# Cross-attention over 16 batches on one Trainium2 core: K and Q projected in transposed form and stacked through DRAM

## The chip, the cores and the metric

The kernel runs on one NeuronCore of a Trainium2 chip, as one launch. The metric is the device time of the launch in microseconds (us), lower is better. The core has a matrix engine (PE, with its weight loads shown apart as PEld), a vector engine (DVE), a scalar engine (ACT), a GpSimd engine (POOL), and a sync engine (SP) that issues most DMA transfers. Each engine runs its own instructions in the order in which they are written; semaphores carry the waits between engines and for transfers.

## The reference

There are 16 batches of 128 query rows (C = 160 channels, 20 heads of D = 8) and 128 context rows (E = 256), of which 124 are text tokens and 4 are image-prompt (IP) tokens. Cut to what matters, for each batch:

```python
q = heads(x @ W_q); k_t = heads(text @ W_k); v_t = heads(text @ W_v)
probs_t = softmax(q k_t^T * D**-0.5); text_out = probs_t v_t
k_ip = heads(ip @ W_k_ip); v_ip = heads(ip @ W_v_ip)
qsem = l2norm(probs_t @ text); sem = qsem . l2norm(ip)
probs_ip = softmax(q k_ip^T * D**-0.5 + 0.5 * sem) * spatial_mask
out = (text_out + probs_ip v_ip) @ W_out + b_out + x
```

## The kernel before, in words

**Windows.** All engines run `windows(...)`: window b = -1 to 18, one per batch, each made of G = 5 groups of HG = 4 heads. Windows 4 to 13 are a hardware loop of pairs; n = 1 - p is the buffer of the next batch, p that of this one. In window b, PE computes the scores of batch b (L706, one matmul of 512 columns for a group: `q_stack` holds 4 heads stacked on 128 partitions, `k_diag` the K of the 4 heads on a block diagonal), transposes the probabilities of two groups back (L723), and multiplies those of three groups back by V and by the Gram matrix of the context (L746, L748, `main_rhs`, from which the norm of qsem comes). DVE takes the row maxima (L627, L628) and the sums of products (L608, L610), ACT the exponentials (L497) and the copy of the transposed probabilities (L466). The IP branch of the batches before runs on POOL: a power for the norm (`rnorm`, L429, the last thing in POOL's window), then in the next window `fused` (L369, L373), the IP output (L248, L253, L256), `text` (L379), `ip_stage` (L385), a copy of IP columns (L389), `centred` (L394), sums, the V columns (L409, L410), `rip_masked` and `ip_probs` (L419, L423). The power waits for `clamped` of DVE (L556), made in group 4.

**K and Q before.** fp32 values are split in a high and a low fp32r part, so that one fp32r matmul with a contraction over 4 heads x 8 channels x 4 products gives the exact scores. In window b, for batch b + 1: PE computes Gram, V and K with the tokens on the partitions (L686, 12 instructions) and Q (L758, 4); ACT copies the high parts (L448, L503), DVE subtracts to get the low parts (L633, L565); PE turns `k_split` and `q_split` with an identity (L765, L775, L713, L714); ACT copies the turned data out of PSUM (L485, L453, L458, L459) into `k_stack` and `q_stack`; SP spreads `k_stack` to the diagonal with eight transfers (L314, L324). `k_diag` and `q_stack` are needed at the score matmul of group 0 in window b + 1.

**SP's order** in a window: IP rows of K (L292), context and x of batch b + 2 (L297, L299), residual rows and V of the IP tokens (L303, L306), `k_diag` groups 0 to 3 (L314), `main_rhs` (L319), `k_diag` group 4 (L324), the output (L329). SP is one in-order queue: a wait holds up every transfer behind it. The work ahead of the windows (the prologue) loads the weights, normalises the IP tokens and projects their K and V; window -1 makes K and Q of batch 0 on chip.

## Time and profile before

| | |
|---|---|
| median of 3 runs | 233.72 us (233.47 to 237.01) |
| profiled execution, device time | 234.08 us |
| its span in the trace | 232.0 us |
| granted PE clock, mean share of full | 0.958 |
| PE busy | 207.8 us, 90% |
| DVE / ACT / POOL busy | 190.8 / 170.0 / 154.4 us |
| DMA, share of 16 engines | 44.6% |

The span is what the trace covers; the device time is 2.1 us longer. "Busy" counts an instruction from start to end, and matmuls overlap in the pipeline, so the chain of waits, where each piece is counted once, gives the truer PE durations. A line number is that of the kernel before unless the text says that it is one of the changed kernel.

### The profile page before, as it was taken

To read this page: it belongs to the slowest core of one execution; us is meant where nothing else is said; L and a number is where in the kernel's file an instruction comes from. 1 tells how busy PE (TensorE), PEld (TensorE's weight loads), DVE (VectorE), ACT (ScalarE), POOL (GpSimd) and SP (SyncE) were. 2 spreads that over 40 slices of the span, in tenths; PEclk is the share of its full clock that TensorE was granted. 3 is DMA by queue.
4 is the path that set the end of the run, shared out by engine and by line. 5 is a ranking of instruction groups with operands and counts; after the bars stand their busy time and mean duration, and the time that the engine had idled before them with its cause. 6 is when DMAs were issued, how large, how long until landed. Compare 5 with 4: busy or idle time off the path is not lost.

```text
span 232.0 us, 6889 instructions
## 1 busy us (share of the span) xinstructions
PE 207.8 (90%) x1562; PEld 192.6 (83%) x1562; DVE 190.8 (82%) x1149; ACT 170.0 (73%) x561; POOL 154.4 (67%) x263
## 2 busy tenths in 40 slices
PE   1948989999999999999999999999999999988433
PEld 1647879998898999999999999999999999977222
DVE  5753778796979798998979897989798979998862
ACT  2063978897978798897969797988888888975000
POOL 5611003649596868788796969696969696979650
PEclk9976999999999999999999999999999999999955
DMA  5405433465355545373736353646454553533030
GB/s 150 124 18 154 104 101 66 124 172 142 104 160 143 149 132 163 87 206 82 204 80 186 104 172 99 167 119 158 132 152 144 145 149 106 143 87 85 1 100 14
DMA packets 46348, 28.57 MB, mean 123 GB/s; under 512 B 7897, under 2 KB 43898, under 8 KB 46330
## 3 DMA queue, kind: packets, MB, share of 16 engines
q1 hardware_dynamic: 46330, 28.38, 44.6%
q8 instruction: 6, 0.10, 0.2%
q14 instruction: 12, 0.10, 0.1%
HBM read 11.11 MB, written 1.52 MB: 54 GB/s over the span
## 4 chain that ended last, share of the span: by engine, by line
PE 61%; DMA 9%; DVE 8%; POOL 7%; ACT 6%; issue 4%; SPq 3%; DVEq 0%; POOLq 0%; ACTq 0%
PE main_ps L746 11%; PE main_ps L748 11%; PE probsT_ps L723 10%; PE pa L686 9%; DMA main_rhs<-g_stage 6%; PE score_ps L706 6%; PE pb L732 5%; POOL rnorm L429 3%; PE pb L758 3%; PE pa L765 2%; ACT probs L497 2%; DVE junk L608 2%; PE pa L775 2%; SPq L324 1%; PE pb L695 1%
## 5 line engine op out<-in xcount | busy, mean ns | idle before, releaser
L497 ACT ACTIVATE probs<-score_ps,negmax 128x124 f32<-128x124 f32 x320 | 93.3, 413 | 0.7 <-DVE negmax L628 0.6
L608 DVE CUSTOM_DVE_ANT_0 junk<-main_ps,probs 128x124 f32<-128x124 f32 x320 | 78.0, 281 | 2.3 <-PE main_ps L748 1.5
L746 PE MATMUL main_ps<-main_rhs,probsT 124*128 124x137 f32 x320 | 65.1, 284 | 1.5 <-DVE small L610 1.4
L748 PE MATMUL main_ps<-main_rhs,probsT 124*128 124x137 f32 x320 | 63.3, 279 | 0.0
L429 POOL TENSOR_TENSOR rnorm<-clamped,exponent 128x20 f32<-128x20 f32 (+1 forms) x16 | 54.8, 3427 | 1.1 <-DVE clamped L556 1.1
L628 DVE TENSOR_REDUCE negmax<-score_ps 128x4 f32<-128x496 f32 x80 | 53.1, 664 | 0.0
L466 ACT ACTIVATE probsT<-probsT_ps 124x512 f32<-124x512 f32 x80 | 51.1, 639 | 2.8 <-PE probsT_ps L723 2.0
L746 PEld LDWEIGHTS main_ps<-main_rhs,probsT 124*128 124x128 f32 x320 | 48.9, 190 | 3.5 <-issue 2.6
L748 PEld LDWEIGHTS main_ps<-main_rhs,probsT 124*128 124x128 f32 x320 | 48.7, 188 | 0.0
L723 PE MATMUL probsT_ps<-ident_sb,probs 128*124 128x128 f32 x320 | 48.2, 273 | 0.0
L723 PEld LDWEIGHTS probsT_ps<-ident_sb,probs 128*124 128x124 f32 x320 | 38.4, 139 | 5.2
L706 PE MATMUL score_ps<-k_diag,q_stack 128*128 128x512 f32 x80 | 39.0, 488 | 0.3 <-ACT probs L497 0.3
L627 DVE COPY ip_score<-score_ps 128x16 f32<-128x16 f32 x80 | 13.3, 166 | 21.4 <-PE score_ps L706 21.4
L610 DVE COPY small<-main_ps 128x26 f32<-128x26 f32 x160 | 28.8, 180 | 0.0
L608 DVE DVE_READ_ACCUMULATOR2_ANT norm<- 128x1 f32 x320 | 26.6, 83 | 0.2 <-issue 0.2
L444 ACT ACTIVATE g_stage<-pa 128x128 f32<-128x128 f32 x16 | 4.4, 278 | 26.5 <-PE pa L686 16.4
L686 PE MATMUL pa<-wkv_sb,ctxT_sb 128*128 128x160 f32 x128 | 21.9, 319 | 0.0
L399 POOL TENSOR_TENSOR ip_exp_half<-ip_exp 128x40 f32<-128x40 f32 x16 | 4.0, 253 | 25.7 <-ACT ip_exp L491 25.7
L686 PEld LDWEIGHTS pa<-wkv_sb,ctxT_sb 128*128 128x128 f32 x128 | 19.8, 208 | 0.0
L248 POOL TENSOR_TENSOR ip_prod<-vrep,ip_probs 128x640 f32<-128x640 f32 x13 | 18.3, 1404 | 0.0
L409 POOL TENSOR_TENSOR main_rhs<-v_stage,one 124x80 f32<-124x80 f32 x16 | 5.1, 321 | 18.9 <-PE main_ps L748 8.9
L732 PE MATMUL pb<-wout_sb,oT 96*128 96x160 f32 x64 | 14.2, 349 | 2.9 <-DVE oT L620 2.9
(91 smaller groups left out, 339.2 us busy)
## 6 DMA issues: line engine op xcount, KB each, us to landing
main_rhs<-g_stage SPq DMA_DIRECT2D x16, 660.0 KB, 4.1
vrep<-vip_d SPq DMA_DIRECT2D x16, 320.0 KB, 3.5
k_diag<-k_stack SPq DMA_DIRECT2D x60, 64.0 KB, 2.1
ctxT_sb<-ctxT SPq DMA_DIRECT2D x16, 124.0 KB, 2.6
xT_sb<-xT SPq DMA_DIRECT2D x16, 80.0 KB, 2.0
xn_sb<-xn SPq DMA_DIRECT2D x16, 80.0 KB, 2.0
out<-out_sb SPq DMA_DIRECT2D x16, 80.0 KB, 1.7
k_diag<-k_stack SPq DMA_DIRECT2D x60, 16.0 KB, 2.0
```

Source lines behind the costliest of these rows:

```text
L429: pool.tensor_tensor(rnorm[:, heads], clamped[:, heads], exponent[:, heads], ALU.pow).then_inc(s_rnorm, 1)
L466: act.activation(probsT[tp][:, :, :].rearrange("t h s -> t (h s)"), probsT_ps[tp][0:T, :], ACT.Copy).then_inc(s_probsT, 1)
L497: last = act.activation(probs[p][:, h, :], score_ps[(p * G + g) % 2][:, j * TOK:j * TOK + T], ACT.Exp, bias=negmax[p][:, h:h + 1])
L608: dve.tensor_tensor_reduce(junk[:, 2 * r + a, :], u, probs[wb][:, h, :], 1.0, 0.0, ALU.mult, ALU.add, norm2[wb][:, h:h + 1])
L610: dve.tensor_copy(small[wb][:, PG * gg + r, :], main_ps[r][:, T:T + SMALL]).then_inc(s_norm, 1)
L628: dve.tensor_reduce(negmax[p][:, HG * g:HG * g + HG], sc[:, :, 0:T], AX_X, ALU.max, negate=True).then_inc(s_max, 1)
L686: mm = pe.matmul(pa[:, lo:lo + width], ctxT_sb[n][:, c, :], r, start=(c == 0), stop=(c == EC - 1))
L706: pe.matmul(score_ps[(p * G + g) % 2][:, :], q_stack[p][:, g, :], k_diag[p][:, g, :, :].rearrange("r h t -> r (h t)"), start=True, stop=Tr ...
L723: mm = pe.transpose(probsT_ps[tp][0:T, j * S:(j + 1) * S], probs[tb][:, HG * tg + j, :], ident_sb[:, :])
L732: mm = pe.matmul(pb[:, 0:C], oT[:, c, :], wout_sb[:, c, :], start=(c == 0), stop=(c == 1))
L746: pe.matmul(main_ps[r][:, 0:MAIN], probsT[mp][:, 2 * r, :], blk[:, RW - MAIN:RW], start=True, stop=True)
L748: pe.matmul(main_ps[r][:, MAIN:2 * MAIN], probsT[mp][:, 2 * r + 1, :], blk[:, 0:MAIN], start=True, stop=True).then_inc(s_main, 1)
```

## The change

- The projections of K and Q now have the weight as the stationary operand and produce channels on the partitions and tokens in the columns, in two halves of 80 channels (`project_k`, `project_q`). They run in group 4 of window b for batch b + 2, into the PSUM bank `pb`. Gram and V (`gram_and_v`) run in group 1 for batch b + 1. The output projection moves to bank `pa`.
- In group 0 of window b, one ACT copy and one DVE subtraction of 80 x 512 make the high and low parts of K and Q of batch b + 1 (`kq_split`). POOL's new `k_columns` writes the four IP columns of K into it, behind `ip_stage` in POOL's order.
- SP stores `kq_split` to DRAM (`store_k` two transfers, `store_q` four), then, after `ctxT` and `xT`, waits for these stores and loads the stacked forms back (`load_k` four transfers to the diagonal, `load_q` one). All of this is in window b, for batch b + 1.
- Gone are the turns on PE, the ACT copies of turned and doubled data, the DVE subtractions on doubled data, the K rows through `kip_d`, and window -1. The prologue is written in a new order; ACT issues two of the weight loads and, for batch 0, `store_q` and `load_q`.

```diff
+        def store_k(eng, n):
+
+            for x in range(2):
+                src = kq_split[:, x, :, :].rearrange("p a t -> p (a t)").bitcast(F32)
+                eng.dma_start(k_d[n, x * CH:(x + 1) * CH, :, :],
+                              src.unsqueeze(1).broadcast_to([CH, 2, 2 * TOK])).then_inc(s_kst, 16)
+
+        def store_q(eng, n):
+
+            for x in range(2):
+                for a in range(2):
+                    eng.dma_start(q_d[n, x * CH:(x + 1) * CH, :, a * S:(a + 1) * S],
+                                  kq_split[:, 2 + x, :, :].bitcast(F32)).then_inc(s_qst, 16)
+
+        def stacked_rows(dram, n, j, rows):
+
+            return bass.AP(dram.tensor, dram.offset + n * G * HG * ROWS * TOK + j * ROWS * TOK,
+                           [[TOK, rows], [HG * ROWS * TOK, G], [1, TOK]])
+
+        def load_k(sp, n):
+            for j in range(HG):
+                sp.dma_start(k_diag[n][ROWS * j:ROWS * (j + 1), :, j, :].bitcast(F32),
+                             stacked_rows(k_d, n, j, ROWS)).then_inc(s_kd[n], 16)
+
+        def load_q(sp, n):
+            sp.dma_start(q_stack[n][:, :, :].bitcast(F32), stacked_rows(q_d, n, 0, HG * ROWS)).then_inc(s_qd[n], 16)
...
                 n = 1 - p
+                if w == 1:
+                    sp.wait_ge(s_vip, 1)
+                    sp.dma_start(vip_d, vip_sb[:, :]).then_inc(s_vip_out, 16)
                 if has(w) and has(w, ahead=1):
 
-                    wait(sp, s_kT, b + 1)
-                    wait(sp, s_kq4, b + 1)
-                    sp.dma_start(k_split[T:TOK, :, :, :, :].rearrange("t h c a d -> t (h c a d)").bitcast(F32),
-                                 kip_d[bass.ds((b + 1) * NIP, NIP), :]).then_inc(s_kip_in, 16)
+                    wait(sp, s_kcol, b + 2)
+                    store_k(sp, n)
+                    store_q(sp, n)
                 if has(w) and has(w, ahead=2):
 
-                    wait(sp, s_ctx_mm, b + 1)
-                    sp.dma_start(ctxT_sb[p][:, :, 0:T], ctxT[b + 2]).then_inc(s_ctx_in[p], 16)
-                    wait(sp, s_q_mm, b + 1)
-                    sp.dma_start(xT_sb[p][0:CH, :, :], xT[b + 2]).then_inc(s_xT_in[p], 16)
+                    wait(sp, s_gv_mm, b + 1)
+                    sp.dma_start(ctxT_sb[p][:, :, NIP:TOK], ctxT[b + 2]).then_inc(s_ctx_in[p], 16)
+                    sp.dma_start(xT_sb[p][:, :, :], xT[b + 2]).then_inc(s_xT_in[p], 16)
+                if has(w) and has(w, ahead=1):
+
+                    wait(sp, s_kst, 32 * (b + 2))
+                    load_k(sp, n)
+                    wait(sp, s_qst, 64 * (b + 2))
+                    load_q(sp, n)
                 if has(w, lag=2):
 
...
+                if has(w) and has(w, ahead=1):
 
...
+                    sp.dma_start(main_rhs[n][:, :, D + 1:D + 1 + WIN],
+                                 g_stage[:, :].unsqueeze(1).broadcast_to([TOK, NPAIR, WIN])).then_inc(s_grep[n], 16)
...
+            def ip_columns(b, p):
+
+                cols = bass.AP(ctxT_sb[p], 0, [[EC * WIN, 128], [WIN, EC], [TOK, 2], [1, NIP]])
+                src = ipunitT[:, :, bass.ds(b * NIP, NIP)].unsqueeze(2).broadcast_to([128, EC, 2, NIP])
+                pool.tensor_copy(cols, src).then_inc(s_ipcol, 1)
+
+            def k_columns(b):
+
+                pool.tensor_copy(kq_split[:, 0:2, :, T:TOK].bitcast(F32),
+                                 kip_split[:, :, :, bass.ds(b * NIP, NIP)].bitcast(F32)).then_inc(s_kcol, 1)
+
...
+                if has(w) and has(w, ahead=1):
+                    wait(pool, s_lo, b + 3)
+                    k_columns(b + 1)
                 if has(w) and has(w, ahead=2):
-                    wait(pool, s_ctx_mm, b + 1)
-                    pool.tensor_copy(ctxT_sb[p][:, :, T:TOK],
-                                     ipunitT[:, :, bass.ds((b + 2) * NIP, NIP)]).then_inc(s_ipcol, 1)
+                    wait(pool, s_gv_mm, b + 1)
...
-                    if g == 0 and has(w, ahead=1):
-
-                        wait(act, s_ctx_mm, b + 2)
-                        if w is None or w >= 0:
-                            wait(act, s_grep[p], 16 * (i + 1))
-                        act.activation(g_stage[:, NIP:NIP + TOK], pa[:, 0:TOK], ACT.Copy)
-                        act.activation(g_stage[:, 0:NIP], pa[:, T:TOK], ACT.Copy).then_inc(s_gstage, 1)
+                    if g == 0 and has(w) and has(w, ahead=1):
+
+                        wait(act, s_kq_mm, b + 3)
+                        wait(act, s_kst, 32 * (b + 1))
+                        wait(act, s_qst, 64 * (b + 1))
+                        act.activation(kq_split[:, :, 0, :], pb[0:CH, :].rearrange("p (x t) -> p x t", x=4),
+                                       ACT.Copy).then_inc(s_hi, 1)
+                    if g == 2 and has(w) and has(w, ahead=1):
+
+                        wait(act, s_gv_mm, b + 2)
+                        wait(act, s_grep[p], 16 * (i + 1))
+                        gv_stage()
                         wait(act, s_vcopy, b + 1)
-                        act.activation(v_stage[:, :], pa[0:T, TOK:TOK + C], ACT.Copy)
-                        act.activation(k_split[0:T, :, :, 0, :], doubled(pa[0:T, TOK + C:TOK + 2 * C]),
-                                       ACT.Copy).then_inc(s_khi, 1)
-                    if g == 3 and has(w) and has(w, ahead=1):
-
-                        wait(act, s_qT, b + 2)
-                        act.activation(q_stack[n][:, 0:G - 1, :].rearrange("r g t -> r (g t)"), pa[:, :],
-                                       ACT.Copy).then_inc(s_qst03, 1)
-                    if g == 4 and has(w) and has(w, ahead=1):
-
-                        wait(act, s_kq4, b + 2)
-                        act.activation(k_stack[:, G - 1, :], pb[:, 0:TOK], ACT.Copy)
-                        act.activation(q_stack[n][:, G - 1, :], pb[:, TOK:TOK + S], ACT.Copy).then_inc(s_st4, 1)
+                        v_stages()
...
-                    if g == 1 and has(w, ahead=1):
-
-                        wait(act, s_kT, b + 2)
-                        if w is None or w >= 0:
-                            wait(act, s_kd03[p], 64 * (i + 1))
-                            wait(act, s_kd4[p], 64 * (i + 1))
...
-                        else:
-                            act.activation(k_stack[:, 0:G - 1, :].rearrange("r g t -> r (g t)"), pa[:, :],
-                                           ACT.Copy).then_inc(s_kst03, 1)
...
+                    if g == 0 and has(w) and has(w, ahead=1):
+
+                        wait(dve, s_hi, b + 3)
+                        dve.tensor_tensor(kq_split[:, :, 1, :], pb[0:CH, :].rearrange("p (x t) -> p x t", x=4),
+                                          kq_split[:, :, 0, :], ALU.subtract).then_inc(s_lo, 1)
                     if has_group(w, g, 4):
...
+            def project_k(bank, n, width):
+
+                for x in range(2):
+                    for c in range(EC):
+                        mm = pe.matmul(bank[0:CH, x * TOK:x * TOK + width], wk_sb[:, c, x * CH:(x + 1) * CH],
+                                       ctxT_sb[n][:, c, NIP:NIP + width], start=(c == 0), stop=(c == EC - 1))
+                return mm
+
+            def project_q(bank, lo, n):
+
+                for x in range(2):
+                    for c in range(2):
+                        mm = pe.matmul(bank[0:CH, lo + x * S:lo + (x + 1) * S], wq_scaled[:, c, x * CH:(x + 1) * CH],
+                                       xT_sb[n][:, c, :], start=(c == 0), stop=(c == 1))
+                return mm
+
+            def gram_and_v(n):
+
+                for lo, width, r in ((0, WIN, ctxT_sb[n]), (WIN, C, wv_sb)):
+                    for c in range(EC):
+                        mm = pe.matmul(pa[0:T, lo:lo + width], ctxT_sb[n][:, c, NIP:TOK], r[:, c, :],
+                                       start=(c == 0), stop=(c == EC - 1))
+                return mm
+
+            pe.wait_ge(s_ctx_in[0], 16)
...
                         if g == 0:
-                            wait(pe, s_kd03[p], 64 * (i + 1))
-                            wait(pe, s_qst03, b + 1)
-                        if g == G - 1:
-                            wait(pe, s_kd4[p], 64 * (i + 1))
+                            wait(pe, s_kd[p], 64 * (i + 1))
+                            wait(pe, s_qd[p], 16 * (i + 1))
...
                             pe.matmul(main_ps[r][:, MAIN:2 * MAIN], probsT[mp][:, 2 * r + 1, :], blk[:, 0:MAIN],
                                       start=True, stop=True).then_inc(s_main, 1)
-                    if g == 0 and has(w, ahead=1):
-
-                        if w == -1:
-                            wait(pe, s_wq, 1)
-                        wait(pe, s_xT_in[n], 16 * (i + p + 1))
+                    if g == 4 and has(w) and has(w, ahead=2):
+
+                        wait(pe, s_ctx_in[p], 16 * (i + 2))
+                        wait(pe, s_xT_in[p], 16 * (i + 2))
+                        wait(pe, s_ipcol, b + 3)
+                        wait(pe, s_lo, b + 3)
+                        project_k(pb, p, TOK)
+                        project_q(pb, 2 * TOK, p).then_inc(s_kq_mm, 1)
+                    if g == 1 and has(w) and has(w, ahead=1):
+
                         wait(pe, s_final, b - 3)
-                        wait(pe, s_st4, b + 1)
-                        for c in range(2):
-                            mm = pe.matmul(pb[:, 0:C], xT_sb[n][:, c, :], wq_scaled[:, c, :], start=(c == 0), stop=(c == 1))
-                        mm.then_inc(s_q_mm, 1)
-                    if g == 1 and has(w, ahead=1):
-
-                        wait(pe, s_klo, b + 2)
-                        wait(pe, s_kip_in, 16 * (b + 2))
-                        for k in range(G - 1):
-                            mm = pe.matmul(pa[:, k * TOK:(k + 1) * TOK], stacked(k_split, k), ident_r_sb[:, :],
-                                           start=True, stop=True)
-                        mm.then_inc(s_kT, 1)
-                    if g == 2 and has(w, ahead=1):
-
-                        wait(pe, s_qlo, b + 2)
-                        if w != -1:
-                            wait(pe, s_kst03, b + 2)
-                        bank_q = main_ps[1] if w == -1 else pa
-                        for k in range(G - 1):
-                            mm = pe.matmul(bank_q[:, k * S:(k + 1) * S], stacked(q_split, k), ident_r_sb[:, :],
-                                           start=True, stop=True)
-                        mm.then_inc(s_qT, 1)
+                        wait(pe, s_vstage, b + 1)
+                        gram_and_v(n).then_inc(s_gv_mm, 1)
```

On SP, in the last window ahead of the loop (window 3; the loop has the same order), the kernel before issues, with its waits:

```order
L292 DMA k_split<-kip_d 4x640 [waits s_kq4,s_kT]
L297 DMA ctxT_sb<-ctxT 128x2x124 [waits s_ctx_mm]
L299 DMA xT_sb<-xT 80x256 [waits s_q_mm]
L303 DMA xn_sb<-xn 128x160
L306 DMA vrep<-vip_d 128x640
L314 DMA k_diag<-k_stack 32x4x128 [waits s_kst03,s_scores]
L314 DMA k_diag<-k_stack 32x4x128 x3
L319 DMA main_rhs<-g_stage 128x10x132 [waits s_gstage,s_main]
L324 DMA k_diag<-k_stack 32x128 [waits s_st4]
L324 DMA k_diag<-k_stack 32x128 x3
L329 DMA out<-out_sb 128x160 [waits s_final]
```

and the changed kernel at the same place (its own line numbers):

```order
L256 DMA k_d<-kq_split 160x1x256 [waits s_kcol]
L256 DMA k_d<-kq_split 160x1x256
L263 DMA q_d<-kq_split 160x1x128 x4
L316 DMA ctxT_sb<-ctxT 128x2x124 [waits s_gv_mm]
L317 DMA xT_sb<-xT 80x256
L273 DMA k_diag<-k_d 32x5x128 [waits s_kst]
L273 DMA k_diag<-k_d 32x5x128 x3
L277 DMA q_stack<-q_d 128x5x128 [waits s_qst]
L329 DMA xn_sb<-xn 128x160
L332 DMA vrep<-vip_d 128x640
L339 DMA main_rhs<-g_stage 128x10x132 [waits s_gstage,s_main]
L344 DMA out<-out_sb 128x160 [waits s_final]
```

The first transfer of SP's window now waits for POOL's `k_columns` (`s_kcol`), twelve transfers stand ahead of and up to the arrival of `q_stack`'s, and a window issues 17 where it issued 14.

On POOL, in the middle of the first window of the loop, the kernel before has (REGISTER_ALU and ISA are bookkeeping of the loop):

```order
L256 TENSOR_TENSOR ip_out<-ip_half 128x160 [waits s_attn,s_ipout]
L379 TENSOR_TENSOR text<-small,rden 128x160 [waits s_attn]
L240 REGISTER_ALU
L240 REGISTER_ALU [waits s_max]
L385 TENSOR_TENSOR ip_stage<-ip_score,one 128x80 [waits s_fuse]
L240 REGISTER_ALU
L389 ISA [waits s_ctx_mm]
L389 COPY ctxT_sb<-ipunitT 128x2x4
L394 TENSOR_TENSOR centred<-fused,ipmax 128x80 [waits s_ipmax]
```

and the changed kernel:

```order
L250 TENSOR_TENSOR ip_out<-ip_half 128x160 [waits s_attn,s_ipout]
L414 TENSOR_TENSOR text<-small,rden 128x160 [waits s_attn]
L234 REGISTER_ALU
L234 REGISTER_ALU [waits s_max]
L420 TENSOR_TENSOR ip_stage<-ip_score,one 128x80 [waits s_fuse]
L234 REGISTER_ALU
L368 ISA [waits s_lo]
L368 COPY kq_split<-kip_split 80x4x4
L364 ISA [waits s_gv_mm]
L364 COPY ctxT_sb<-ipunitT 128x2x2x4
L431 TENSOR_TENSOR centred<-fused,ipmax 128x80 [waits s_ipmax]
```

The copy that releases SP's stores stands where the copy of the context's IP columns stood, behind the power of the window before and the whole IP output.

## Rows read from the trace of the kernel before

**Rows 1.** Windows view: stretch, busy us (instructions) by engine, granted clock, DMA.
```profile
core 0: us, PE busy (x) PEld busy (x) DVE busy (x) ACT busy (x) POOL busy (x), PEclk, DMA share, GB/s
103.33:115.36 12.03, 12.03 (x100) 11.57 (x99) 10.86 (x73) 10.49 (x37) 9.69 (x17) 1.00 0.54 144
```

**Rows 2.** Chain of waits from 103 us: start us, us, engine, tile, line.
```profile
103.33 1.53 PE pa L686 x12
104.87 0.23 PE score_ps L706
...
106.48 0.55 PE pb L758 x4
...
108.63 0.40 PE pa L765 x4
109.03 0.28 PE score_ps L706
...
110.68 0.40 PE pa L775 x4
...
113.80 0.06 PE pb L713
113.86 0.11 PE pb L714
...
115.36 1.53 PE pa L686 x12
116.90 0.23 PE score_ps L706
```

**Rows 3.** Timeline of window 8: start us, us, engine, line, operation.
```profile
124.85 0.11 DVE L556 TENSOR_TENSOR clamped<-norm,guard 128x20 f32<-128x20 f32 x1
125.41 3.54 POOL L429 TENSOR_TENSOR rnorm<-clamped,exponent 128x20 f32<-128x20 f32 x1
```

**Rows 4.** Timeline, SP's issues and POOL's column copy, same window.
```profile
118.91 0.64 SPq L297 DMA_DIRECT2D ctxT_sb<-ctxT  x1
...
119.74 0.45 SPq L299 DMA_DIRECT2D xT_sb<-xT  x1
...
120.44 0.35 SPq L303 DMA_DIRECT2D xn_sb<-xn  x1
...
121.24 0.19 POOL L389 COPY ctxT_sb<-ipunitT 128x8 f32 x1
...
121.90 2.60 SPq L314 DMA_DIRECT2D k_diag<-k_stack  x4
```

**Rows 5.** DMA view, issues by tile: count, KB each, median us to landing.
```profile
main_rhs<-g_stage SPq DMA_DIRECT2D x16, 660.0 KB, 4.1
vrep<-vip_d SPq DMA_DIRECT2D x16, 320.0 KB, 3.5
k_diag<-k_stack SPq DMA_DIRECT2D x60, 64.0 KB, 2.1
xT_sb<-xT SPq DMA_DIRECT2D x16, 80.0 KB, 2.0
```

**Rows 6.** Lines view: shapes, count, busy us, mean ns, idle before.
```profile
L453 ACT ACTIVATE q_stack<-pa 128x512 fp32r<-128x512 f32 x15 | 10.0, 667 | 0.0
L633 DVE TENSOR_TENSOR k_split<-pa,k_split 124x320 fp32r<-124x320 f32 x16 | 7.8, 489 | 4.4 <-ACT k_split L448 4.4
```

**Rows 7.** Timeline of PE: first score matmul of windows 0, 3 and 15.
```profile
19.64 0.83 PE L706 MATMUL score_ps<-k_diag,q_stack 128*128 128x512 f32 x1
...
54.16 0.50 PE L706 MATMUL score_ps<-k_diag,q_stack 128*128 128x512 f32 x1
...
199.71 0.48 PE L706 MATMUL score_ps<-k_diag,q_stack 128*128 128x512 f32 x1
```

**Rows 8.** Windows view of short stretches; columns as in Rows 1.
```profile
14.00:15.00 1.00, 0.30 (x3) 0.16 (x2) 0.56 (x2) 0.95 (x3) 0.00 (x0) 0.71 0.00 0
...
34.00:35.00 1.00, 0.00 (x0) 0.00 (x0) 1.00 (x9) 0.00 (x0) 0.00 (x0) 1.00 0.79 203
```

More of the change, by code:

```diff
@@ L36 @@
 CH = C // 2
-CP = 96
+CR = CH + 1
+WIN = NIP + TOK
+ROWS = 4 * D
 HG = 4
@@ L211, in xattn_program @@
         block = ctx.enter_context(nc.Block())
-        def doubled(cols):
-            r = cols.rearrange("t (h d) -> t h d", d=D)
-            return r.unsqueeze(2).broadcast_to([r.shape[0], H, 2, D])
         def windows(eng, window):
-            for w in range(-1, 4):
+            for w in range(4):
                 window(w, w % 2, w // 2, w)
@@ L675, in window @@
                     grp = b * G + g
-                    if g == 0 and has(w, ahead=1):
-                        wait(pe, s_ctx_in[n], 16 * (i + p + 1))
-                        wait(pe, s_ipcol, b + 2)
-                        if w == 0:
-                            wait(pe, s_kst03, 1)
-                        wait(pe, s_qst03, b + 1)
-                        for lo, width, rhs in ((0, TOK, None), (TOK, C, 0), (TOK + C, C, C)):
-                            for c in range(EC):
-                                r = ctxT_sb[n][:, c, :] if rhs is None else wkv_sb[:, c, rhs:rhs + C]
-                                mm = pe.matmul(pa[:, lo:lo + width], ctxT_sb[n][:, c, :], r, start=(c == 0), stop=(c == EC - 1))
-                        mm.then_inc(s_ctx_mm, 1)
                     if g == 3 and has(w, lag=3):
```

312 lines of the change are left out of this document (154 added, 158 removed).

## The prediction

> **What bounds the kernel now.** I read the windows view first, to see whether one engine is full: from 103 to 115 us, one window, PE is busy throughout, at full clock, and DVE, ACT and POOL have about 1.2, 1.6 and 2.4 us of slack in 12 [rows 1]. Then the chain of waits, to see what the window is made of. It has nothing but PE from one L686 group to the next: 115.36 - 103.33 = 12.03 us [rows 2]. So the body is PE-bound, and from the score matmul of window 3 (54.16) to that of window 15 (199.71) it takes 145.55 us, 12.13 a window [rows 7]. Ahead of window 0 lie 19.6 us, behind the start of window 15 another 232.0 - 199.7 = 32.3 us, where the power on POOL and the output of the last batches run down.
>
> The other thing to read is how late K and Q of the next batch may come. Now they never leave the chip's engines except for the spread to `k_diag`. The question for the changed kernel is whether its longer way, POOL, SP, DRAM and back, still ends before the next window's first score matmul.
>
> **PE, what goes and comes.** Gone in a window: L686 1.53, Q 0.55, turns 0.40 + 0.40 + 0.06 + 0.11, together 3.05 us [rows 2]. L686's 12 instructions stream 4 x 128 + 8 x 160 = 1792 columns in 1.53 us, 0.85 ns a column. The new ones: K 8 x 128, Q 8 x 128, Gram 4 x 132, V 4 x 160 = 3216 columns, 2.75 us. Net -0.30 us. Two score matmuls behind the turns cost 0.28 instead of 0.23 in the same chain; taken as gone too, a full PE would need 12.03 - 0.4 = 11.65 us, call it 11.7.
>
> **ACT and DVE.** ACT loses seven copies and gains one of 80 x 512, as L453's 0.67 us; DVE loses two of 0.49 us and gains one of 512 columns, about 0.7 [rows 6]. Neither was the bound, so both are costed at nothing; PE's 12.03 us hides them.
>
> **The way of K and Q, which sets the window.** T is the start of a window's first score matmul (116.90 for window 8, 104.87 for window 7, from the chain [rows 2, 4]). Step by step:
> 1. T to `clamped` on DVE: 124.96 - 116.90 = 8.1 us; the power starts at 125.41, T + 8.5 [rows 3]. Nothing that the change removes lies between PE's third group and DVE's fourth except 0.05s.
> 2. The power, 3.54 us, then `fused` twice, the IP output, `text`, `ip_stage`. The column copy behind them starts at 121.24, that is 121.24 - 104.87 = 16.4 us behind the T of the window before [rows 4]. `k_columns` stands at this very place. I take 16.2, since DVE has one subtraction less in the way, plus 0.2 for the copy itself.
> 3. SP: six stores, `ctxT`, `xT`, four loads, and only then the load of `q_stack`. Four static issues of `k_diag` take 2.60 us, 0.65 each; `ctxT` to `xT` is 0.83, `xT` to `xn` 0.70 [rows 4]. Six stores at 0.63 make 3.8, then 1.5, then 2.6, with gaps 8.0 us. The two waits on stores cost nothing: the last store is issued 3.2 us in and needs about 2.0 to land, as `xT`, while SP is busy with issues until 7.9 us.
> 4. Landing of `load_q`, 320 KB in 512-byte pieces. No row shows that shape. `vrep` with 320 KB takes 3.5; on the line from `xT` (80 KB, 2.0) to `main_rhs` (660 KB, 4.1, pieces of 528 bytes) it would be 2.9 [rows 5]. I take 3.2, plus 0.1 to PE.
>
> Sum: 16.2 + 0.2 + 8.0 + 3.3 = 27.7 us. It leads from T of window b to T of window b + 2, since the power that it contains is that of window b and the copy stands in window b + 1. Two PE-bound windows last 23.4. So the way is 4.3 us too long, and it is a loop: a later T makes a later `clamped`. The window becomes 27.7 / 2 = 13.85 us, with PE idle for 2.15 us ahead of each first score matmul. What else could be late then is not: `ctxT` for the group-4 projection is issued 4.0 us behind the copy, about T + 6.7, and is wanted at T + 10.
>
> The Trainium skill, "DMA: Bandwidth & Descriptors", section "Anatomy of one DMA", gives 2.0 us fixed plus the bytes at 436 GB/s for a transfer (measured on the GpSimd path); by that estimate `load_q` would land in 2.75 us instead of 3.2, and the result would be some 3 us lower. Its "Rules for kernel authors" says that under 64 KB one pays mostly overhead, which speaks against cutting this way in 12 transfers; the trace agrees in that 64 KB takes 2.1 us and 660 KB only 4.1 [rows 5].
>
> **The prologue.** First issues are spread over two queues, so the first K projection should start near 3.5 us (one issue of about 0.6 and a landing of 2 to 3 [rows 4, 5] behind the start), `k_columns` near 7.4 behind eleven short steps on PE, ACT, DVE and POOL, stores to 8.7, loads of K to about 13; ACT stores Q from 9 and can load it only at 13.2, with a landing of 3.3. First score matmul about 16.5 us instead of 19.64 [rows 7]. Window 1 needs `k_columns` in window 0 (16.7) + 8.0 + 3.3 = 28.1, window 2 about 39.3, window 3 the first power: 28.1 + 8.5 + 3.6 + 1.6 + 0.2 + 11.3 = 53.2, against 54.16 now. The gain at the start is thus used up but for 1 us.
>
> **Sum.** Windows 3 to 15: 12 x 13.85 = 166.2 against 145.55, +20.6 us. Start -1.0. Behind T of window 15 POOL is no longer behind, -0.8. Span 232.0 + 18.8 = 250.8, device time 252.9. The profiled execution was 0.4 us above the median of the runs (234.08 against 233.72), so 252.5 in terms of the median; I say 253.
>
> **Rivals.**
> - *The load comes in time (faster).* The way takes under 23.4 us, PE stays full at 11.7 a window. Then T of window 3 is near 51.5, window 15 at 51.5 + 12 x 11.7 = 192, and the time 192 + 32.3 + 2.1 = 226 us. It decides at 23.4 us: step 3 and 4 together would have to be 7.0 us instead of 11.3. SP's short issues take 0.45 (`xT`'s own [rows 4]); ten of those, 1.5 for `ctxT` and `xT` and 2.9 for landing are 4.5 + 1.5 + 2.9 = 8.9. So only with an error in steps 1 and 2 as well. 10 in 100.
> - *Shorter issues, half the stall.* With these 8.9 us the way is 25.3, the window 12.7, and the time T3 = 49.5, + 152 + 31.5 + 2.1 = 235 us: within 2% of before. 10 in 100.
> - *The clock falls as well.* PE's granted clock fell to a mean of 0.71 in the microsecond from 14 us, in which PE was busy for 0.3 us, but it stayed at 1.00 through an idle microsecond at 34 to 35 us [rows 8]. If 2.1 us of idling in every window brings it down to 1.2 GHz for some of the following groups, PE's three groups in step 1 (5.8 us at full clock) take up to 1.7 us more, the way 29.1 to 29.4, the window 14.6, the time about 262 us. 20 in 100. The Trainium skill, "TensorE: Matmul & The Clock Gate", section "HAM oscillation", describes just this, a kernel that waits for a transfer in each tile and runs cold each time; the row at 34 us shows one short wait that did not do it.
> - *DMA engines fill up.* The change adds about 1 MB to some 1.8 MB a window; they are 54% busy now [rows 1], so about 80% after. Not a bound, but landing may rise by a few tenths: inside the range.
>
> **How the numbers follow.** My forecast, stall of about 2 us a window with full clock, 60 in 100: 246 to 258. Low end of the whole 237, near the second rival, high end 262 by the clock. Faster by over 2% 0.10, within 2% 0.10, slower 0.80 (2% is about what a measurement of this kernel can tell from no change).
>
> **What would show it.** Right: the window lasts 13.5 to 14.2 us; PE's longest wait is at the score matmul of group 0, for DMA `q_stack<-q_d`, about 2 us, 12 or more times; on SP the issue of `q_d`'s load stands 7.5 to 8.3 us behind `k_columns`; and `k_columns` starts 16 us behind T of the window before. Wrong: PE full in the middle at 11.7 us a window; or `k_columns` much earlier than the power lets it, or issues on SP well under 0.6 us, or another engine at the end of PE's waits. The first score matmul should be near 16.5 us.

## The result, and the profile after

| | before | changed kernel |
|---|---|---|
| median | 234.26 us (4 runs, 233.47 to 237.01) | 297.13 us (4 runs, 294.72 to 297.56) |
| span of the profiled execution | 232.0 us | 295.3 us |
| PE busy | 207.8 us, 90% | 222.9 us, 75% |
| granted PE clock, mean | 0.958 | 0.932 |

The ratio is 1.268 (95% interval 1.258 to 1.277). The sign was forecast, the size was not: 297 us lies far outside 237 to 262.

The page of the changed kernel, its busy times, the shares of the chain, and two groups with the wait ahead of them:

```profile
PE 222.9 (75%) x1534; PEld 198.6 (67%) x1534; DVE 184.2 (62%) x1125; ACT 154.0 (52%) x468; POOL 153.9 (52%) x276
...
SPq 31%; DMA 22%; PE 14%; POOL 13%; issue 10%; DVE 5%; ACT 1%; POOLq 1%; ACTq 1%; DVEq 0%
DMA vrep<-vip_d 15%; SPq L263 11%; SPq L273 7%; SPq L256 5%; POOL ip_prod L242 5%; SPq L316 3%; DMA q_stack<-q_d 3%; POOL rnorm L462 2%; PE main_ps L780 2%; POOL text L414 2%; SPq L317 2%; PE main_ps L782 2%; PE pa L686 2%; PE probsT_ps L74
...
L619 DVE TENSOR_TENSOR kq_split<-pb,kq_split 80x512 fp32r<-80x512 f32 x15 | 10.3, 687 | 73.9 <-ACT kq_split L508 73.9
...
L242 POOL TENSOR_TENSOR ip_prod<-vrep,ip_probs 128x640 f32<-128x640 f32 x13 | 18.2, 1403 | 65.9 <-DMA vrep<-vip_d 65.9
```

The middle of the chain before was all PE [rows 2]. Now PE holds 14% of it; SP's issues (SPq) and landings hold 53%. The largest single entry is a transfer of which the change moves only the place in SP's queue: `vrep`, the IP tokens' V of an older batch. POOL waits for it at `ip_prod` in all of its 13 uses, 5.1 us each.

The DMA part of the page (KB each, median us from issue to landing) answers to [rows 5]. `main_rhs` and `vrep`, unchanged in size, land 1.9 and 0.9 us later than before; `k_diag` (now 80 KB) and `q_stack` come within 0.1 us of the row before and of the forecast:

```profile
main_rhs<-g_stage SPq DMA_DIRECT2D x16, 660.0 KB, 6.0
...
k_diag<-k_d SPq DMA_DIRECT2D x64, 80.0 KB, 2.2
vrep<-vip_d SPq DMA_DIRECT2D x16, 320.0 KB, 4.4
...
q_stack<-q_d SPq DMA_DIRECT2D x15, 320.0 KB, 3.3
```

First score matmuls, in the timeline of PE, windows 0, 8 and 9. They answer to [rows 7]; the bracket is the idle time before and what ended it:

```profile
20.14 1.19 PE L738 MATMUL score_ps<-k_diag,q_stack 128*128 128x512 f32 x2 [3.49 <-DMA q_stack<-q_d]
...
127.14 0.79 PE L738 MATMUL score_ps<-k_diag,q_stack 128*128 128x512 f32 x1 [1.45 <-DMA q_stack<-q_d]
...
144.05 0.49 PE L738 MATMUL score_ps<-k_diag,q_stack 128*128 128x512 f32 x1 [1.45 <-DMA q_stack<-q_d]
```

Window 0 starts at 20.1 and window 3 at 57.3, against 19.64 and 54.16 before. From window 4 (74.8) to window 14 (246.6) the kernel takes 17.2 us a window, where 13.85 was forecast. Window 3 is the first in which POOL has an `ip_prod`, the reader of `vrep`, and it is the first of the long ones.

The chain of waits of one window of the changed kernel (start us, us, what) shows the ring:

```profile
133.23 0.14 POOL kq_split L368
133.38 0.61 SPq L256
...
134.69 0.60 SPq L263
...
137.43 0.61 SPq L316
...
138.22 0.45 SPq L317
...
138.80 0.35 SPq L273
...
140.69 0.38 SPq L277
...
141.28 0.36 SPq L329
...
141.91 4.53 DMA vrep<-vip_d
...
146.61 1.39 POOL ip_prod L242
...
149.51 0.47 POOL text L414
149.98 0.36 POOL ip_stage L420
150.34 0.14 POOL kq_split L368
150.50 0.60 SPq L256
```

POOL's `k_columns` (L368) releases SP. SP issues six stores (L256, L263), `ctxT` and `xT` (L316, L317), five loads (L273, L277) and `xn` (L329): 8.5 us until it comes to `vrep` at 141.91. `vrep` lands 4.5 us later. `ip_prod` starts with it at 146.61, and behind `ip_prod` in POOL's order stand `ip_half`, `ip_out`, `text`, `ip_stage` and the next `k_columns`, 3.7 us later. From 133.38 to 150.50 it is 17.12 us, and every round of it is one window. PE does not appear in it at all.

One sign that the prediction gave is answered by these lines. `k_columns` was to start 16 us behind the first score of the window before; it starts at 133.23, that is 23.5 us behind that score at 109.76.

### The profile page after: what moved, and what is told of

Read it like the earlier page. It is cut to its first block, busy times and chain, and to the rows that moved or that the text cites. A ratio compares the mean times of both kernels' runs of the same rounds, so it can differ in the third digit from the quotient of the medians.

```text
span 295.3 us, 6714 instructions
## 1 busy us (share of the span) xinstructions
PE 222.9 (75%) x1534; PEld 198.6 (67%) x1534; DVE 184.2 (62%) x1125; ACT 154.0 (52%) x468; POOL 153.9 (52%) x276
## 2 busy tenths in 40 slices
DMA packets 73564, 44.31 MB, mean 150 GB/s; under 512 B 8745, under 2 KB 71498, under 8 KB 73546
## 4 chain that ended last, share of the span: by engine, by line
SPq 31%; DMA 22%; PE 14%; POOL 13%; issue 10%; DVE 5%; ACT 1%; POOLq 1%; ACTq 1%; DVEq 0%
DMA vrep<-vip_d 15%; SPq L263 11%; SPq L273 7%; SPq L256 5%; POOL ip_prod L242 5%; SPq L316 3%; DMA q_stack<-q_d 3%; POOL rnorm L462 2%; PE main_ps L780 2%; POOL text L414 2%; SPq L317 2%; PE main_ps L782 2%; PE pa L686 2%; PE probsT_ps L748 2%; PE score_ps L738 2%
## 5 line engine op out<-in xcount | busy, mean ns | idle before, releaser
L535 ACT ACTIVATE probs<-score_ps,negmax 128x124 f32<-128x124 f32 x320 | 90.1, 370 | 16.4 <-DVE negmax L654 15.2
L780 PE MATMUL main_ps<-main_rhs,probsT 124*128 124x137 f32 x320 | 68.0, 295 | 5.6 <-DVE small L636 5.5
L782 PE MATMUL main_ps<-main_rhs,probsT 124*128 124x137 f32 x320 | 65.3, 286 | 0.0
L780 PEld LDWEIGHTS main_ps<-main_rhs,probsT 124*128 124x128 f32 x320 | 51.6, 200 | 8.4 <-issue 3.4
L619 DVE TENSOR_TENSOR kq_split<-pb,kq_split 80x512 fp32r<-80x512 f32 x15 | 10.3, 687 | 73.9 <-ACT kq_split L508 73.9
L748 PE MATMUL probsT_ps<-ident_sb,probs 128*124 128x128 f32 x320 | 51.5, 287 | 0.0
L782 PEld LDWEIGHTS main_ps<-main_rhs,probsT 124*128 124x128 f32 x320 | 51.0, 196 | 0.0
L748 PEld LDWEIGHTS probsT_ps<-ident_sb,probs 128*124 128x124 f32 x320 | 42.3, 146 | 7.1 <-issue 1.5
L670 PE MATMUL pb<-ctxT_sb,wk_sb 128*80 128x128 f32 (+1 forms) x128 | 19.7, 304 | 28.1 <-DMA xT_sb<-xT 22.1
L670 PEld LDWEIGHTS pb<-ctxT_sb,wk_sb 128*80 128x80 f32 x128 | 16.3, 168 | 30.4 <-issue 23.8
L738 PEld LDWEIGHTS score_ps<-k_diag,q_stack 128*128 128x128 f32 x80 | 16.4, 206 | 27.2 <-issue 22.1
L508 ACT ACTIVATE kq_split<-pb 80x512 fp32r<-80x512 f32 x15 | 8.9, 593 | 44.8 <-PE pb L678 44.8
L653 DVE COPY ip_score<-score_ps 128x16 f32<-128x16 f32 x80 | 13.2, 165 | 15.9 <-PE score_ps L738 15.8
L757 PE MATMUL pa<-wout_sb,oT 81*128 81x160 f32 x64 | 14.4, 352 | 4.6 <-DVE oT L646 4.1
```

The source lines that it names most:

```text
L535: last = act.activation(probs[p][:, h, :], score_ps[(p * G + g) % 2][:, j * TOK:j * TOK + T], ACT.Exp, bias=negmax[p][:, h:h + 1])
L670: mm = pe.matmul(bank[0:CH, x * TOK:x * TOK + width], wk_sb[:, c, x * CH:(x + 1) * CH], ctxT_sb[n][:, c, NIP:NIP + width], start=(c == 0), ...
L738: pe.matmul(score_ps[(p * G + g) % 2][:, :], q_stack[p][:, g, :], k_diag[p][:, g, :, :].rearrange("r h t -> r (h t)"), start=True, stop=Tr ...
L748: mm = pe.transpose(probsT_ps[tp][0:T, j * S:(j + 1) * S], probs[tb][:, HG * tg + j, :], ident_sb[:, :])
L780: pe.matmul(main_ps[r][:, 0:MAIN], probsT[mp][:, 2 * r, :], blk[:, RW - MAIN:RW], start=True, stop=True)
L782: pe.matmul(main_ps[r][:, MAIN:2 * MAIN], probsT[mp][:, 2 * r + 1, :], blk[:, 0:MAIN], start=True, stop=True).then_inc(s_main, 1)
```

## The experiments

Every experiment changes only the order of instructions, but for one that adds a wait; all of them compute the whole result. Line numbers are those of the changed kernel, shifted by the few lines of an edit. The letters in the expectations:
- **A**: the ring above, one window long, through `vrep`; behind it the ring of K and Q that I had forecast, two windows long.
- **B**: the K/Q way alone sets the window, only longer than I sized it. Where an expectation has a **C**, that rival sees nothing in the place of these transfers.
- **D** (formed after the first experiments): a third ring, over DVE's new subtraction; in the last two expectations the ring that is then left, over POOL's wait for that subtraction. **E**, in two of them: the way of K and Q over SP is still what ends last.

**`vrep` ahead of SP's wait.** In SP's window, the loads of `xn` and `vrep` go ahead of the wait for `k_columns`:

```diff
+                if has(w, lag=2):
+                    ...
+                    sp.dma_start(vrep[p][:, :, :, :].rearrange("s m h d -> s (m h d)"), ...
                 if has(w) and has(w, ahead=1):
 
                     wait(sp, s_kcol, b + 2)
                     store_k(sp, n)
```

> The changed kernel with one edit: in SP's window the loads of the residual rows and of vrep stand ahead of the wait for k_columns instead of behind the load of q_stack. Theory A: the changed kernel's window of 17.1 us is a loop one window long: k_columns, SP's thirteen issues and that of vrep (8.5 us), vrep's landing (4.5), ip_prod to the next k_columns (3.7 + 0.2). Without vrep in it the loop is gone and the longer way of K and Q, two windows long, is left: 16.2 + 0.2 + 7.3 + 3.4 = 27.1 us, so a window of 13.6, and 250 to 256 us in all. Rival B: the way of K and Q itself sets the 17.1 us and vrep's lateness only follows it: the window stays 17.1 and the time 297. Rival C: the transfer engines are the limit, since the kernel moves 44 MB instead of 29: the same bytes, so 297 as well.

Measured: 259.75 us, ratio 1.107 [1.097, 1.117]. Moving these two loads gives back 37 of the 63 us, so the rivals, by which `vrep` does not matter, fall. It is 4 us above the 250 to 256 expected. Windows 3 to 9 last between 12.6 and 16.7 us, only windows 10 to 13 13.6 to 14.0, and the mean of windows 4 to 13 is 14.1. From window 11 on the chain is the one that I had forecast (chain of waits of this kernel); in window 9 it passes over ACT's copy and DVE's subtraction (143.72 and 144.34) instead:

```profile
189.38 0.15 POOL kq_split L368
189.54 0.61 SPq L256
...
196.94 3.15 DMA q_stack<-q_d
...
200.32 0.50 PE score_ps L738
...
208.94 3.54 POOL rnorm L462
...
213.33 1.36 POOL ip_prod L242
```

First score matmuls stand at 186.37, 200.32 and 214.22: 27.85 us for two windows, where the sum of steps 1 to 4 was 27.7; over windows 4 to 13 two windows take 28.3 us on average.

**`k_columns` at the head of POOL's window**, ahead of `fused` and the IP output. It needs only DVE's subtraction:

```diff
+                if has(w) and has(w, ahead=1):
+                    wait(pool, s_lo, b + 3)
+                    k_columns(b + 1)
                 if has(w, lag=2):
 
                     wait(pool, s_rnorm, b if w == B + 1 else b - 1)
```

> The changed kernel with one edit: k_columns stands at the head of POOL's window, ahead of fused and the IP output, instead of behind ip_stage. Theory A: k_columns no longer waits for vrep in the same window, so the one-window loop is broken; vrep's lateness now closes a loop of two windows: SP 8.5, landing 4.6, ip_prod to the start of the power 8.5, the power 3.6, the copy 0.2, together 25.4, a window of 12.7 and about 240 us. Rival B (only K and Q's own way counts): T to the power 8.5, power 3.6, copy 0.2, SP 7.3, landing 3.4, together 23.0, PE full at 11.7 and about 228 us. Rival C (transfer engines): 297.

Measured: 253.73 us, ratio 1.084 [1.073, 1.095]. By the orders it opens both rings, since neither the IP output nor the power of the window before stands ahead of SP any more. But it came out 13 us above what A gave for it, with a window of 13.74 us.

**Both at once.**

> The changed kernel with both edits, the loads of residual rows and vrep ahead of the wait for k_columns on SP, and k_columns at the head of POOL's window. Theory A: neither loop is left that is longer than PE's own work; the way of K and Q is 23.0 us for two windows, so the window is 11.7 to 12.0 us and the time 227 to 233 us, a little under the kernel before. Rival C (transfer engines or queue load): clearly above, since the bytes are all still there.

Measured: 254.71 us, ratio 1.086 [1.076, 1.095], 22 us above what A gave. The same 13.74 us a window (126.17, 139.92, 153.65), so there is a third bound that I had not named. C, which said "clearly above" here, is not yet excluded. The waits view of this kernel (us in total, times, longest):

```profile
DVE kq_split L619 <- ACT kq_split L508: 46.0, 15, 7.2
POOL kq_split L368 <- DVE kq_split L619: 32.4, 15, 6.8
PE main_ps L780 <- DVE small L636: 18.5, 17, 1.4
```

`q_stack` is no longer late; DVE is. The timeline of the same kernel around the head of a window says why:

```profile
124.27 0.40 PE L782 MATMUL main_ps<-main_rhs,probsT 124*128 124x137 f32 x2
...
126.17 0.48 PE L738 MATMUL score_ps<-k_diag,q_stack 128*128 128x512 f32 x1
...
126.61 0.59 ACT L508 ACTIVATE kq_split<-pb 80x512 fp32r<-80x512 f32 x1 [1.06 <-PE pb L678]
...
127.24 0.69 DVE L619 TENSOR_TENSOR kq_split<-pb,kq_split 80x512 fp32r<-80x512 f32 x1 [2.85 <-ACT kq_split L508]
...
127.85 0.27 DVE L634 CUSTOM_DVE_ANT_0 junk<-main_ps,probs 128x124 f32<-128x124 f32 x1
```

PE projects K and Q as the last thing in its window. ACT can copy only then, and DVE's subtraction stands first in its own window, so DVE sits idle for 2.85 us, although the products behind it in its order (L782) are done at 124.67. It catches up too late for PE, which waits for `small` (the bank that DVE must free) some 1.1 us at a time.

**`ctxT` and `xT` ahead of the wait**, `vrep` left where it was. It takes two issues, about 1.4 us, out of the ring and nothing else:

```diff
+                if has(w) and has(w, ahead=2):
+                    wait(sp, s_gv_mm, b + 1)
+                    sp.dma_start(ctxT_sb[p][:, :, NIP:TOK], ctxT[b + 2]).then_inc(s_ctx_in[p], 16)
+                    sp.dma_start(xT_sb[p][:, :, :], xT[b + 2]).then_inc(s_xT_in[p], 16)
                 if has(w) and has(w, ahead=1):
 
                     wait(sp, s_kcol, b + 2)
```

> The changed kernel with one edit: the loads of context and x of batch b + 2 stand ahead of the wait for k_columns, so that 1.4 us of issues less lie between k_columns and vrep, and between k_columns and the load of q_stack. Theory A (a loop of one window): each window is 1.4 us shorter, 15.7 us, and the time about 279 us. Rival B (the way of K and Q over two windows): 0.7 us a window, about 288 us. Rival C (transfer engines): no change, 297.

Measured: 283.62 us, ratio 1.206 [1.194, 1.219]. The time alone does not choose: it lies midway between the 279 of A and the 288 of B. The windows and the chain do. Windows 7 to 13 last 15.8 us on average against 17.1, 1.2 us less, where a ring of two windows would give 0.7; windows 4 and 5 are longer (17.1 and 16.5), and behind the last first score the kernel takes 35.1 us instead of 33.2. The chain of waits of this kernel has `vrep` once in every window, and one round of it takes 15.8 us:

```profile
127.53 0.15 POOL kq_split L368
...
134.95 4.59 DMA vrep<-vip_d
...
143.35 0.14 POOL kq_split L368
```

**All three moves.**

> e3_both with the loads of context and x of batch b + 2 also ahead of the wait for k_columns. e3_both came out at 254.7 us and a window of 13.74, though neither loop through SP should have been longer than 12. Theory D: its windows are set by the place of the split: ACT's copy and DVE's subtraction of kq_split stand first in group 0, but PE ends the projections only as the last thing of the window before, so DVE stands still for 3.1 us a window with the sums of products behind it, and PE's next products wait for DVE. Then moving context and x changes nothing: 253 to 255 us. Rival E (the way of K and Q over SP is still what ends last): 1.4 us of issues less gives 0.7 to 1.4 us a window, 236 to 245 us. Rival C (transfer engines, 70% busy in e3_both): 254.

Measured: 254.06 us, ratio 1.082 [1.074, 1.090]; no gain over the two moves, window 13.74 again. The way of K and Q is not what is left.

**All three, and DVE's subtraction moved** behind the sums and maxima of group 0:

```diff
-                    if g == 0 and has(w) and has(w, ahead=1):
-
-                        wait(dve, s_hi, b + 3)
-                        dve.tensor_tensor(kq_split[:, :, 1, :], pb[0:CH, :].rearrange("p (x t) -> p x t", x=4),
-                                          kq_split[:, :, 0, :], ALU.subtract).then_inc(s_lo, 1)
...
+                    if g == 0 and has(w) and has(w, ahead=1):
+
+                        wait(dve, s_hi, b + 3)
+                        dve.tensor_tensor(kq_split[:, :, 1, :], pb[0:CH, :].rearrange("p (x t) -> p x t", x=4),
+                                          kq_split[:, :, 0, :], ALU.subtract).then_inc(s_lo, 1)
                     if g == 2 and w == 0:
```

> e6_all_three (254.1 us) with DVE's subtraction for kq_split moved from the head of group 0 to behind that group's sums of products and maxima; PE, ACT, POOL and SP keep their orders. Theory D, as e7_project_g3 left it: what sets the 13.7 us is that DVE stands still for ACT's copy with the sums of group 0 behind it, which PE's next products wait for; wherever PE projects, the copy on ACT comes late. With the sums ahead DVE loses only some 0.6 us a window, PE is full at 11.7 to 12.2 us a window, and the time is 230 to 237 us. Rival C (transfer engines, 70% busy): 254, since the bytes are the same. Rival E (K and Q's way, which this makes some 0.3 us later): 254 or more.

Measured: 241.44 us, ratio 1.034 [1.030, 1.037], 12.6 us less than without the move by the medians, 11.4 by the two ratios, 11.9 by twelve windows of 12.75 instead of 13.74 us (132.46 to 145.14 to 157.94): about 12 us. It is 4 us above the expected range. The kernel moves the same bytes as the changed kernel, 44.31 MB, so C falls here. DVE no longer waits for ACT ahead of `kq_split` in its windows. POOL's wait for DVE's subtraction, 32.1 us before the move, is now the longest:

```profile
POOL kq_split L368 <- DVE kq_split L654: 41.7, 15, 8.4
```

**That move alone**, in the changed kernel as it was:

> The changed kernel with only DVE's subtraction moved behind the sums and maxima of group 0. Theory A: the loop of one window through vrep is the longest by 3 us, so nothing that happens on DVE can show: 294 to 298 us. If the stall of DVE is added to the loop rather than hidden in it, about 1.5 us a window less, 275 us.

Measured: 297.41 us, ratio 1.271 [1.264, 1.278]: nothing. The same edit is worth about 12 us or none, by whether a longer ring lies over it.

**Projections one group earlier.** I tried to cure the third ring at its source: on top of all three moves, PE projects at the end of group 3 instead of 4.

```diff
-                    if g == 4 and has(w) and has(w, ahead=2):
+                    if g == 3 and has(w) and has(w, ahead=2):
```

> e6_all_three with the projections of K and Q for batch b + 2 at the end of group 3 of PE's window instead of group 4; nothing else moves. Theory D: they are then ready some 2.3 us before ACT and DVE come to the split at the head of the next window, DVE's wait for ACT's copy falls from 3.1 to under 1 us a window, PE is full again at 11.7 to 12.1 us a window, and the time is 229 to 235 us. Rival C (transfer engines): the same bytes at the same busy share, so 250 us or more.

Measured: 267.41 us, ratio 1.139 [1.130, 1.147], a clear miss: 13 us worse. The orders read as follows (this reading was not tested by itself): ACT's order was not moved with it. Its copy still stands in the next window behind the exponentials of group 4, whose scores the projections now delay. DVE waits 33 us in place of 46 for the copy, but PE waits 27.0 instead of 20.7 us for `small`. With DVE's subtraction moved as well:

> e7_project_g3 (267.4 us) with the same move of DVE's subtraction. There ACT's copy stood behind the exponentials of group 4, whose scores the projections in group 3 had delayed. Theory D: as in e9_lo_behind_max DVE is free, so this too falls to 230 to 240 us. If the place of the projections itself costs (PE's products of group 4 and the exponentials 1.8 us later), it stays well above e9_lo_behind_max, at 245 or more.

Measured: 247.72 us, ratio 1.064 [1.061, 1.067], against 241.44 with the projections in group 4. So the place itself costs 6 us.

**The first window.** On top of the projections in group 3, SP holds back the 660 KB copy into `main_rhs` of batch 0 until `load_q` has landed:

```diff
             sp.wait_ge(s_gstage, 1)
+            sp.wait_ge(s_qd[0], 16)
```

> e7_project_g3 with one wait more in the prologue: SP issues the 660 KB copy into main_rhs for batch 0 only when q_stack of batch 0 has landed. In the changed kernel that load, issued on ACT's queue at 14.5 us, landed after 5.5 us instead of 3.3, beside the 660 KB of SP's queue. If the two queues share the transfer engines and that is the delay, the first score matmul comes at about 18 us instead of 20, and the time is some 1 to 2 us under e7_project_g3; if the first group was held up by something else, no change.

Measured: 268.37 us, ratio 1.142 [1.134, 1.149], no gain over 267.41, where 1 to 2 us were expected. But it bears on what delayed the first score. The added wait holds back not the copy alone: `wvip` (160 KB) and two small loads stand behind it on SP. Timeline of PE in this kernel:

```profile
17.42 1.19 PE L739 MATMUL score_ps<-k_diag,q_stack 128*128 128x512 f32 x2 [1.91 <-DMA q_stack<-q_d]
22.23 1.33 PE L764 MATMUL main_ps<-wvip_sb,ipT_sb 128*64 128x160 f32 x4 [3.63 <-DMA wvip_sb<-wvip]
```

The first score comes at 17.4 us, against 19.7 without the added wait and 20.1 in the changed kernel, near the 16.5 forecast, and the time is lost again behind `wvip`, which SP now issues later.

**POOL's idle stretch.** In the kernel at 241.44 us POOL waits 1.84 us at the head of its window for DVE (timeline of that kernel), and the chain of waits runs over this wait, `ip_prod`, `ip_out`, DVE's `attn_out` and PE's output projection to the next subtraction:

```profile
134.47 0.19 POOL L368 COPY kq_split<-kip_split 80x16 f32 x1 [1.84 <-DVE kq_split L654]
```

Two places for `k_columns` fill it: behind `ip_prod`, or between `fused` and `ip_prod`.

> On top of the kernel with the three loads and the K columns ahead and DVE's low parts behind the maxima (241.44 us, window 12.8): POOL copies the K columns only behind ip_prod, so that it does not idle 1.84 us at the head of its window. Theory D (the ring that is left runs over POOL's idle stretch: DVE's low parts, K columns, fused, ip_prod, ip_out, DVE attn_out, PE's output projection): ip_prod starts up to 1.2 us earlier, and the next bound is the K/Q way within one window: first score to low parts 1.9, K columns 0.5 late, stores and loads 9.4, matmul 0.2, a window of 12.0 to 12.2, so 229 to 233 us, at or below the kernel before (233.4 in these studies). Rival (POOL's idle stretch was not on the ring, or PE at 11.9 plus small waits is the floor already): 240 to 242.

> The same, but the K columns stand between the two fused additions and ip_prod: only the 0.7 us of the two fused instructions move into POOL's idle stretch, and nothing of the K/Q way gets later. Theory D: the window falls by at most 0.7 us to 12.1 to 12.4, so 230 to 236 us; if it is as fast as the placement behind ip_prod, the K/Q way is the next bound, if it is slower by some 6 us, POOL's stretch was. Rival: 240 to 242.

Measured: 240.06 us, ratio 1.027 [1.020, 1.033], and 238.14 us, ratio 1.021 [1.015, 1.026]. Both are above what D gave, and the first lies in the rival's range. In both the window does fall to 12.2 us (131.21, 143.39, 155.64 in the second), but not at once. With `k_columns` behind `ip_prod`, windows 3 to 5 took 13.5 to 14.5 us: POOL was late there, and the chain carries its lateness over SP to `q_stack`. So both expectations held for the steady window (12.0 to 12.2, and 12.1 to 12.4) and missed the way there. With `k_columns` ahead of `ip_prod`, only windows 3 and 5 are long (12.7 and 13.5). This kernel is the best version found, and it still is 2% behind the kernel before: its first score is at 20.25 instead of 19.64, windows 0 to 2 last 1.2 us longer, windows 3 to 14 another 2.3 us (147.9 against 145.6).

Its windows view, one window, shows why little more is to be had by such moves; it answers to [rows 1]:

```profile
118.94:131.21 12.27, 12.16 (x99) 11.24 (x97) 10.64 (x69) 9.44 (x29) 10.02 (x18) 1.00 0.78 223
```

PE is all but full again, at 12.16 of 12.27 us. In the timeline its stream has one clear hole of about 0.3 us, ahead of the output projection. With that taken off the 12.2, a full PE needs, by estimate, some 11.9 us a window with the new projections, against 12.03 before.

## Why the prediction was right in sign and wrong in size

- **The ring that was forecast exists, near its size, but it did not set the time of the changed kernel.** The way of K and Q is longer than two PE-bound windows and closes into a loop. With `vrep` out of the way it measured, against the forecast: first score to power 8.6 (8.5), first score to the end of `k_columns` 16.9 (16.4), from there to the issue of `load_q` 7.4 (8.0), landing and start of PE 3.4 (3.3, and not the 2.75 of the other estimate); two windows 27.85 (27.7). The 8.5 and 16.4 start at 116.90 and 104.87, where the chain has the score; the timeline has it at 116.63 and 104.60, and by the timeline, as in the measured values, they would be 8.8 and 16.6. Yet the 13.9 us window is no clean proof: the third ring would hold it at 13.74 anyway, and no run has the K/Q way alone. The chain and PE's nine waits for `q_stack` in that kernel, 16.1 us, are what shows the K/Q way at work.
- **The step that failed** is the sentence behind the sum of the K/Q way, "What else could be late then is not". I looked at `ctxT` there, and not at what stands behind `load_q` in SP's queue: `xn` and `vrep`. Before, SP issued `vrep` right behind `xn`, ahead of `k_diag`. The change puts a wait for POOL and eleven new issues ahead of it, and what waits for `vrep` is POOL, ahead of the very `k_columns` that releases SP. The sum was to be had: 8.0 for the issues, 0.6 for `xn`, 3.5 for the landing of `vrep` [rows 5], and 3.6 for POOL from `ip_prod`, in the timeline of the kernel before, to the column copy at 121.24 [rows 4], with 0.1 for the copy:

```profile
117.64 1.41 POOL L248 TENSOR_TENSOR ip_prod<-vrep,ip_probs 128x640 f32<-128x640 f32 x1
```

  That is 15.8 us in a single window, longer than 13.85. Over the 12 windows from 3 to 15 it is 12 x 1.95 = 23 us on top of the 253 forecast, 276 us. The other 1.3 us of a window are 1.0 of longer landing (4.5) and 0.3 of gaps. The rival on full DMA engines gave landings "a few tenths" more; in this ring the landing counts in full, so its 1.0 is 12 us in twelve windows. Of the 44 us between 253 and 297, the windows from 3 to 15 make 38.6, the later start of window 3 (57.3 instead of 53.2) 4.1 and the end 1.7.
- **ACT and DVE "costed at nothing".** This was wrong by about 12 us, but hidden under the other two rings. Each of the two instructions is short (0.59 and 0.69 us, forecast 0.67 and 0.7). Their place was not looked at: both wait for the last instructions of PE's window, and stand first in their engines' orders.
- **PE.** New projections plus Gram and V came to 2.74 us in a chain, 0.99 for Gram and V, 0.88 and 0.87 for K and Q (forecast 2.75). The full window is about 11.9 instead of 11.7.
- **The prologue.** First score at 20.1, forecast 16.5. The term that failed is the landing of the first `load_q`: 5.5 us instead of 3.3, beside the 660 KB copy and `wvip` on SP's queue. A further 1.3 us lie in the steps before: its issue at 14.5 instead of 13.2.
- **The clock rival.** It did fall, in six of the ten windows from 4 to 13 (0.84 to 0.95 over a window), but this was not the cause of the time: the other four had 1.00 and last 16.6 to 17.6 us like the six, and the ring over `vrep` does not pass through PE.
- **The rivals with a faster load** had 20 in 100 and were wrong: issues of loads from DRAM were indeed short (0.35 to 0.44 us), those of the six stores were not (0.60 to 0.61). The way has eleven transfers, not the twelve that the prediction names, and the smallest is 80 KB, so the remark there on transfers under 64 KB does not reach them.

## What to carry to other kernels

When a wait and a row of issues are put into an in-order queue, list every transfer behind them, not only those that the change is about, and ask of each whether its reader stands ahead of the releaser of that wait: if so, it is a ring, and its length in windows sets the price. Remove one ring and look again before judging an edit, since the same move was worth nothing or about 12 us here. A short instruction that waits for another engine's last result cost those 12 us at the head of DVE's window: look at where it stands, not only at how long it takes.

## What the runs showed of the hardware

- **A landing depends on what else is under way, also from another queue.** The first `load_q` (320 KB, issued by ACT) took 5.5 us in the changed kernel beside the 660 KB copy and the 160 KB of `wvip`, both issued by SP, 5.2 us in the kernel with the projections in group 3, and 3.3 us when these were held back there. No run tells the copy's share from that of `wvip`. Rows of the DMA view from 8 us on, of the changed kernel and then of the one that holds them back:

```profile
q_stack<-q_d ACTq DMA_DIRECT2D x1, 320.0 KB, 5.5
```

```profile
q_stack<-q_d ACTq DMA_DIRECT2D x1, 320.0 KB, 3.3
```

  The Trainium skill, "Trainium Kernel Development and Optimization", section "Key Constraints", says that transfers issued from several engines' queues share the same 16 DMA engines, and that a second queue saves only issue time. These two rows agree with the shared engines; on the issue time they say nothing.
- **Issue time depends on the transfer.** On SP's queue the six stores out of SBUF took 0.60 to 0.61 us each, the four loads of `k_diag` from DRAM 0.35 to 0.44, `load_q` 0.38.
- **The clock after a stall.** In the changed kernel PE stood idle for 1.45 us ahead of both scores shown above. At the second the granted clock was 1.00. At the first it was 0.50, and it had fallen already between 125 and 126 us, while PE was still projecting and ahead of that idle stretch; it stayed at about 0.50 until 132 us. Between these two windows PE's other wait differs, the one for `xT` ahead of the projections: 2.02 us in the first case, 0.72 in the second. But that wait alone does not decide it. In window 11 it was 2.92 us, with 1.63 us ahead of the score behind it, and the clock stayed at 1.00. What decides it stays open.

```profile
123.54 1.07 PE L670 MATMUL pb<-ctxT_sb,wk_sb 128*80 128x128 f32 x8 [2.02 <-DMA xT_sb<-xT]
...
140.66 1.07 PE L670 MATMUL pb<-ctxT_sb,wk_sb 128*80 128x128 f32 x8 [0.72 <-DMA xT_sb<-xT]
...
208.22 1.07 PE L670 MATMUL pb<-ctxT_sb,wk_sb 128*80 128x128 f32 x8 [2.92 <-DMA xT_sb<-xT]
...
211.80 0.49 PE L738 MATMUL score_ps<-k_diag,q_stack 128*128 128x512 f32 x1 [1.63 <-DMA q_stack<-q_d]
```

  The windows view in single microseconds, columns as in [rows 1]:

```profile
125.00:126.00 1.00, 0.68 (x5) 0.31 (x3) 0.00 (x0) 0.12 (x1) 0.00 (x0) 0.58 0.96 258
...
126.00:127.00 1.00, 0.00 (x0) 0.00 (x0) 0.50 (x1) 0.47 (x1) 0.00 (x0) 0.50 0.45 141
...
143.00:144.00 1.00, 0.00 (x0) 0.00 (x0) 0.57 (x1) 0.40 (x1) 0.00 (x0) 1.00 0.96 197
...
211.00:212.00 1.00, 0.20 (x1) 0.21 (x2) 1.00 (x4) 0.00 (x0) 0.00 (x0) 1.00 1.03 192
```

  The window from 127.14 to 144.05 has a mean clock of 0.86 and PE busy for 14.59 us, the next one 0.95 and 12.79 us, and both last 17 us: the clock's price, up to 1.8 us of PE's time, was wholly covered by the ring.
